# Third layer: the decays over the running sum computed once for 32 heads and broadcast to each tile by DMA

## The reference, cut to what matters

```
dt    = softplus(dt + dt_bias);  Adt = -exp(A_log) * dt          # one number per head and position
A_cum = cumsum(Adt) inside a chunk
Y_diag= (C B^T * exp(segsum(Adt))) @ h                           # inside a chunk
Y_off = (C @ state of the chunks before) * exp(A_cum)            # from the chunks before
y     = Y_diag + Y_off + D * h
g     = y * silu(gate);  out = rmsnorm(g) @ W_out + b_out
```

## Time and profile before

| | |
|---|---|
| median of 3 runs | 1292.9 us (1292.6 to 1293.01) |
| the profiled execution's own time | 1296.16 us |
| its span, first to last instruction | 1294.4 us |
| mean granted TensorE clock | 0.961 |
| busy: PE, weight loads | 1150.9 us (89%), 615.3 us (48%) |
| busy: DVE, ACT, POOL | 939.9 us (73%), 795.5 us (61%), 573.9 us (44%) |
| DMA | 68.48 MB, mean 53 GB/s |

### The profile page before, as it was taken

The page is one execution under the profiler, slowest core; times in us unless marked ns, Lnnn a source line. Parts: engine busy times, 40 slices in busy tenths (PEclk is TensorE's granted clock), DMA queues, the critical chain, the costliest instruction groups (busy, mean ns, idle before and its releaser), DMA issues.

```text
span 1294.4 us, 14453 instructions
## 1 busy us (share of the span) xinstructions
PE 1150.9 (89%) x4948; PEld 615.3 (48%) x4948; DVE 939.9 (73%) x1361; ACT 795.5 (61%) x1089; POOL 573.9 (44%) x310
## 2 busy tenths in 40 slices
PE   5777999999989999998489999999999999797887
PEld 1332344444344444444266666666666666322554
DVE  4667999999955545345689999998999999323354
ACT  4567666767543334226668888888888888335542
POOL 9002899898816756230014544554454455300000
PEclk8889999999989999898699999999999999798999
DMA  3001555555422111100000000000000000000000
GB/s 121 1 1 58 192 197 178 191 180 180 174 105 82 50 41 41 41 21 0 2 15 15 15 21 15 15 22 15 15 14 22 16 15 8 1 0 1 1 1 33
DMA packets 31111, 68.48 MB, mean 53 GB/s; under 512 B 6101, under 2 KB 12022, under 8 KB 30774
## 3 DMA queue, kind: packets, MB, share of 16 engines
q1 hardware_dynamic: 31038, 67.56, 16.1%
HBM read 65.25 MB, written 1.51 MB: 52 GB/s over the span
## 4 chain that ended last, share of the span: by engine, by line
PE 41%; DVE 30%; ACT 15%; issue 7%; POOL 6%; DMA 1%; DVEq 0%; SPq 0%; POOLq 0%; ACTq 0%
DVE work L1542 7%; DVE work L1561 6%; DVE work L656 4%; PE ps L1006 4%; PE ps L1196 4%; PE ps L1022 3%; PE ps L1014 3%; POOL work L717 3%; ACT work L1403 3%; DVE yd L1606 3%; ACT work L1398 3%; PE ps L1237 2%; DVE work L1609 2%; PE ps L437 2%; ACT ps L553 2%
## 5 line engine op out<-in xcount | busy, mean ns | idle before, releaser
L1670 POOL TENSOR_TENSOR ssum<-ssum,rs 128x1024 f32<-128x1024 f32 x32 | 77.1, 2410 | 221.3 <-DVE work L1542 219.0
L656 DVE TENSOR_TENSOR_SCAN work<-ps,work 128x1024 f32<-128x1024 f32 x64 | 146.6, 2291 | 8.3
L1542 DVE SCALAR_TENSOR_TENSOR work<-work,w_t 128x1024 f32<-128x1024 f32 x96 | 123.3, 1285 | 24.0 <-ACT work L1403 21.7
L437 PE MATMUL ps<-work,ident 128*128 128x512 f32 x256 | 121.7, 598 | 5.6 <-POOL work L717 5.4
L996 POOL TENSOR_TENSOR work<-work,ssum 128x1024 f32<-128x1024 f32 x32 | 76.2, 2388 | 110.1 <-DVE work L1085 57.7
L1085 DVE TENSOR_TENSOR work<-work,ps 128x512 f32<-128x512 f32 x64 | 43.8, 687 | 99.8 <-PE ps L1014 99.8
L553 ACT ACTIVATE ps<-work,A 128x1024 f32<-128x1024 f32 x64 | 71.6, 1118 | 72.4 <-DVE work L656 72.3
L1064 ACT ACTIVATE work<-ps 128x512 f32<-128x512 f32 x64 | 38.1, 597 | 115.4 <-PE ps L1006 115.4
L717 POOL TENSOR_TENSOR work<-work 128x1024 f32<-128x1024 f32 x42 | 99.1, 2362 | 13.6 <-DVE work L656 12.3
L1678 POOL TENSOR_TENSOR yd<-yd,work 128x896 f32<-128x896 f32 x32 | 67.1, 2097 | 70.7 <-DVE work L1609 70.7
L1585 DVE SCALAR_TENSOR_TENSOR work<-work,ps 128x64 f32<-128x64 f32 x384 | 79.4, 275 | 6.3
(11 more groups left out here) (347 smaller groups left out, 2587.5 us busy)
## 6 DMA issues: line engine op xcount, KB each, us to landing
work<-bc_rows SPq DMA_DIRECT2D x42, 512.0 KB, 3.5
yd<-bc_rows SPq DMA_DIRECT2D x22, 512.0 KB, 3.6
rs<-w_rows SPq DMA_DIRECT2D x32, 256.0 KB, 4.2
ssum<-share_rows SPq DMA_DIRECT2D x32, 256.0 KB, 3.2
w_t<-in_tile_w SPq DMA_DIRECT2D x32, 195.5 KB, 2.4
work<-in_w SPq DMA_DIRECT2D x1, 2048.0 KB, 7.9
shared<-in_f SPq DMA_DIRECT2D x3, 512.0 KB, 6.1
work<-in_x SPq DMA_DIRECT2D x4, 256.0 KB, 3.7
```

The lines of the kernel that those rows point to most:

```text
L437: mm = pe.matmul(ps[:, YACC + h, :], ident[:, :], HS[u % 4][:, h * BL:(h + 1) * BL], start=(n == 0), stop=(n == DS - 1))
L656: dve.tensor_tensor_scan(h, flat_pair(DABANK), h, 0.0, ALU.mult, ALU.add).then_inc(m0["scan"], 1)
L1542: c = dve.scalar_tensor_tensor(HC[u], HP[:, tap:tap + SEQ], par(u, "taps", tap), HC[u], ALU.mult, ALU.add)
L1670: pool.tensor_tensor(ssum[:, b, :], ssum[:, b, :], rs[:, :, :].rearrange("p k t -> p (k t)"), ALU.add).then_inc(m2["ss"], 1)
```

## The change

- `spread_sums` (PE, two matmuls per tile), `decays_out` (ACT, one exponential of 128x896 per tile) and the selector `sel2` with its memset and three selections are gone, and with them PE's wait on `sdo` ahead of `within_chunks`.
- Ahead of the loop ACT computes the exponential of the transposed running sums once, in four instructions of 32x512, into `rtf[0:32]`. They stand behind the copies of the middle parts, and the high part's copies are issued up to two blocks earlier. The fourth stands ahead of `pad_h(0, 0)`.
- SP stores `rtf[0:32]` into a DRAM scratch `sdo_rows` in two DMAs (one per sequence), and for each tile issues two DMAs that broadcast one row of 896 numbers each to 64 partitions of `Y`. In the loop these wait for `outp` and `sqr` of the tile that had that half of `Y` before, and they stand ahead of `load_tile(n + 2)` and `load_rows(n + 2)` on the queue.
- DVE's L1609 waits for the landing of these DMAs and no longer for ACT.

```diff
+            def store_decays(b):
+                sp.wait_ge(m2["sdo"], (b + 1) * NB // BATCH)
+                here = slice(b * SEQ, (b + 1) * SEQ)
+                sp.dma_start(sdo_rows[:, here], rtf[0:H2, here]).then_inc((m2["sdo_rows0"], m2["sdo_rows1"])[b], 16)
+
+            def load_decays(n):
+
+                b, t = divmod(n, CT)
+                if n >= 2:
+                    sp.wait_ge(m2["outp"], n - 1)
+                    sp.wait_ge(m2["sqr"], n - 1)
+                for h in range(2):
+                    sp.dma_start(Y[n % 2][h * P2:(h + 1) * P2, P:],
+                                 sdo_rows[2 * t + h:2 * t + h + 1, b * SEQ + P:(b + 1) * SEQ].to_broadcast([P2, SEQ - P])).then_inc(
+                                     (m2["sdo_in0"], m2["sdo_in1"])[n % 2], 16)
+
             load_tile(0)
             load_tile(1)
+            store_decays(0)
             sp.wait_ge(m2["rows_const"], 1)
             sp.wait_ge(m2["act"], m2["neg"] + NB)
             load_rows(0)
             load_rows(1)
+            store_decays(1)
+            sp.wait_ge(m2["sdo_rows0"], 16)
+            load_decays(0)
+            load_decays(1)
+            sp.wait_ge(m2["sdo_rows1"], 16)
             for n in range(CT * BATCH - 2):
+                if n >= 1:
+                    load_decays(n + 1)
                 sp.wait_ge(m2["hc"], n + 1)
                 sp.wait_ge(m2["wo"], n + 1)
                 load_tile(n + 2)
                 sp.wait_ge(m2["arg"], 4 * n + 4)
                 load_rows(n + 2)
+            load_decays(CT * BATCH - 1)
...
-            def spread_sums(n, b, t):
-
-                pe.wait_ge(m2["L"], 4 * n + 4)
-                for h in range(2):
-                    mm = pe.matmul(ps[:, BACK + h, :], sel2[:, 2 * t:2 * t + 2, :].rearrange("k a p -> k (a p)"),
-                                   parts[:, b * SEQ + h * BL:b * SEQ + (h + 1) * BL], start=True, stop=True)
-                mm.then_inc(m2["sdo_mm"], 1)
...
             def within_chunks(n):
-                pe.wait_ge(m2["sdo"], n + 1)
                 pe.wait_ge(m2["M"], n + 1)
...
-            def decays_out(n, u):
-                act.wait_ge(m2["sdo_mm"], n + 1)
-                if n >= 2:
-                    act.wait_ge(m2["outp"], n - 1)
-                    act.wait_ge(m2["sqr"], n - 1)
-                act.activation(Y[u][:, P:], flat2(BACK)[:, P:], ACT.Exp).then_inc(m2["sdo"], 1)
...
+            def middle(k):
+                act.wait_ge(m2["mid"], k + 1)
+                act.activation(blk(parts[32:64, :], k), part_tmp[0:H2, k % 2, :], ACT.Copy).then_inc(m2["act"], 1)
+                act.activation(blk(rtf[0:H2, :], k), ps[0:H2, 4 + k, :], ACT.Exp).then_inc(m2["sdo"], 1)
...
-            for k in range(NB):
-                act.wait_ge(m2["pe"], m2["cumT"] + 1)
+            act.wait_ge(m2["pe"], m2["cumT"] + 1)
+            for k in range(NB):
                 act.activation(blk(parts[0:32, :], k), ps[0:H2, 4 + k, :], ACT.Copy).then_inc(m2["act"], 1)
-                act.wait_ge(m2["mid"], k + 1)
-                act.activation(blk(parts[32:64, :], k), part_tmp[0:H2, k % 2, :], ACT.Copy).then_inc(m2["act"], 1)
+                if k >= 1:
+                    middle(k - 1)
+            middle(NB - 1)
             pad_h(0, 0)
...
-                dve.wait_ge(m2["sdo"], n + 1)
+                dve.wait_ge((m2["sdo_in0"], m2["sdo_in1"])[u], 32 * (n // 2 + 1))
                 dve.wait_ge(m2["yoff"], 2 * n + 2)
...
-            for t in (ident_b, mask_q, zero, sel, sel2):
+            for t in (ident_b, mask_q, zero, sel):
                 pool.memset(t[:, :] if len(t.shape) == 2 else t[:, :, :], 0.0)
...
-            for t, w in ((sel2, P2), (sel, P)):
-                for k in range(3):
...
+            for k in range(3):
+                ins = pool.affine_select(sel[:, :, :], sel[:, :, :], [[-1, H2], [0, P]], ALU.not_equal, 1.0,
+                                         base=-H2 * k, channel_multiplier=1)
```

More of the change, by code:

```diff
@@ L147, in build @@
         sel = selectors[0:96, :, :]
-        sel2 = sb("sel2", [96, H2, P2], BF16)
         selr2 = sb("selr2", [4 * E, E, HE], BF16)
@@ L215, in build @@
                     dve="row:1 dt_biased:1 bc_conv:2 dt:1 adt:1 acum:1 dec_sub:1 parts:4 bc_conv1:2 gt_out:4 s_out:4",
-                    each="mid bc_pad bc_tap w_in0 w_in1 h_mm h_pad h_tap g_mm sg conv hc tr hdt hdd rows_const rows0 rows1 arg L sdo_mm sdo st first_state rec M yoff ydiag yd ystar y_sum y sqr ss wo outp first_out")
+                    each="mid bc_pad bc_tap w_in0 w_in1 h_mm h_pad h_tap g_mm sg conv hc tr hdt hdd rows_const rows0 rows1 arg L sdo sdo_rows0 sdo_rows1 sdo_in0 sdo_in1 st first_state rec M yoff ydiag yd ystar y_sum y sqr ss wo outp first_out")
         f2 = stages("f2", pe="logit:1 picked_T:1 y:4", act="sig:1 y_out:4 g:4", dve="picked:1 x_out:4", each="rt_out h gelu wbc hw")
@@ L224, in build @@
         share_rows = nc.dram_tensor("share_rows", [E, T], F32, kind="Internal").ap()
+        sdo_rows = nc.dram_tensor("sdo_rows", [H2, T], F32, kind="Internal").ap()
         bc_rows = nc.dram_tensor("bc_rows", [2 * DS, T], F32, kind="Internal").ap()
@@ L1147, in build @@
         STAIRS = 12
+        HI_AT, MID_AT = (1, 2, 4, 6), (3, 5, 7, 8)
         two = lambda k: ps[:, k:k + 2, :]
@@ L1292, in step @@
                     shares(m, b1, 1)
-                    spread_sums(m, b1, t1)
                 if t == 0:
@@ L1353, in l2_pe @@
             shares(0, 0, 1)
-            spread_sums(0, 0, 0)
             pe.wait_ge(m2["dve"], m2["gt_out"] + NB)
@@ L1474, in step @@
             def step(n, b, t, u):
-                decays_out(n, u)
                 more = n + 1 < CT * BATCH
@@ L1529, in l2_dve @@
                 r, tb = rs[0:H2, k % 2, :], part_tmp[0:H2, k % 2, :]
-                dve.wait_ge(m2["act"], m2["hi_mid"] + 2 * k + 1)
+                dve.wait_ge(m2["act"], m2["hi_mid"] + HI_AT[k])
                 own(dve.tensor_tensor(r, ps[0:H2, 4 + k, :], blk(parts[0:32, :], k), ALU.subtract))
@@ L1533, in l2_dve @@
                 dve.wait_ge(m2["mid"], k + 1)
-                dve.wait_ge(m2["act"], m2["hi_mid"] + 2 * k + 2)
+                dve.wait_ge(m2["act"], m2["hi_mid"] + MID_AT[k])
                 dve.tensor_tensor(blk(parts[64:96, :], k), r, tb, ALU.subtract).then_inc(m2["dve"], 1)
@@ L1979, in _ @@
             pool.affine_select(mask_q[:, :], mask_q[:, :], [[-1, P]], ALU.is_ge, -BIG, base=0, channel_multiplier=1)
-            for t, w in ((sel2, P2), (sel, P)):
-                for k in range(3):
[L1983 to L1988, removed]
+            for k in range(3):
+                ins = pool.affine_select(sel[:, :, :], sel[:, :, :], [[-1, H2], [0, P]], ALU.not_equal, 1.0,
+                                         base=-H2 * k, channel_multiplier=1)
+                if k == 2:
+                    ins.then_inc(const["ready"], 1)
+                else:
+                    own(ins)
             l0_pool(pool, own)
```

## The result

The changed kernel takes 1299.58 us (median of 19 runs, 1295.03 to 1302.87) against 1293.82 us (19 runs, 1288.72 to 1297.63) on the same chips: ratio 1.0038, 95% interval 1.0027 to 1.0049. It is slower by some 0.4%; the forecast was 1279.1 us, faster. The profiled execution took 1302.87 us, its span 1301.2 us. What happened is by its mechanism the rival "the weights come late and the kernel is slower", at a smaller size than its 1316.5 us.

The account below looks back on a forecast made before the run. The loop's step was taken to be bound by a chain through PE, ACT and DVE, with spread_sums a link. Terms -13.0 - 1.4 + 0.6 = -13.8 us took 1292.9 to 1279.1 us; own range 1276 to 1282, 8 in 10 1275 to 1287.

Parts of the forecast that it names:

- the weights come late and the kernel is slower: Rival, SP queue in the loop: weights land at X = 5.92 us, step 14.89 us, 1316.5 us in all; chance 0.05.
- What bounds a step: Third layer's loop: a 14.02 us step is a chain through PE, ACT and DVE, with spread_sums a link, decays_out not.
- PE without spread_sums: PE in the loop: project_h starts 0.42 us earlier in 31 tiles, -13.0 us.
- the two long steps with the clearing of the accumulator save the same: Loop steps that clear the accumulator: led by project_h too, so each saves the same 0.42 us.
- DVE's new wait: DVE L1609 in the loop: decays have 14.0 us and land 3.5 us after issue, so it costs nothing.
- What is queued behind on SP: SP queue in the loop: next tile's weights, behind the decay loads, land 0.4 us inside the budget; cost nothing.
- X: Time from sum_out's end to the weights' landing: taken as 4.2 us, budget 4.63; when over it, step is 8.97 + X.
- "a little late" rival: SP queue in the loop: weights land at X = 4.82 us, step 13.79 us, 1284.6 us in all; chance 0.14.
- The prediction's second estimate of X: SP queue: from 2.0 us fixed plus bytes over 436 GB/s, after 0.84 us of issuing, X of 3.5 to 4.4 us.
- The start: Program start: less POOL work lets DVE's fourth L260 end at 25.2 us instead of 28.2; -1.4 us, bounds 0 and -3.0.
- Ahead of the loop: ACT before the loop: the fourth exponential, a 32x512 pass, stands right ahead of pad_h(0, 0); +0.6 us.
- The sum: Whole kernel: -13.0 - 1.4 + 0.6 = -13.8 us, from 1292.9 to 1279.1 us.

Follow-up runs that it names:

- with the weights first: Changed kernel with SP issuing load_tile and load_rows ahead of load_decays in each iteration: 1279.57 us, ratio to before 0.9883; repeated, 1278.41 us, ratio 0.9884.
- the wait alone: Changed kernel loading decays for tiles 0 and 1 only, SP's wait for outp and sqr kept ahead of load_tile: 1281.9 us, step 13.59 us.

## Why the prediction was wrong

- **What bounds a step:** right. A chain through PE, ACT and DVE, `spread_sums` a link, `decays_out` not. Both were put back alone and did what was said (14.02 and 13.59 us).
- **PE without spread_sums, 0.42 us for 31 tiles:** right as a size, 14.02 - 13.59 = 0.43 us. In the changed kernel only the second step shows it; with the weights first every usual step does. That "the two long steps with the clearing of the accumulator save the same" was wrong for the one of step 16, 16.50 us in both: PE's wait of 0.50 us for ACT L1488 ahead of L1266 takes in what the matmuls leave.
- **DVE's new wait:** right, no wait of DVE for a decay load appears in the list.
- **What is queued behind on SP, "cost nothing, with a thin margin":** this is the step that failed. The mechanism, the cycle 8.97 + X and the point from which it costs (X of 5.05) were right; X was mis-sized, 4.2 us for a measured 5.35 in the step shown (median 5.24). Three parts of it: the two issues and the gap took 1.25 us, where I took 0.92 from loads of 128 partitions; the weights landed 3.96 us after their own issue (median 3.8), where I had 3.24; and PE's start behind the landing (0.14 us) was left out. Besides, PE's part of the step is 9.07 us for 8.97, because project_h takes 1.96 us for 1.88 when it starts on the landing; that its first weight load can no longer run ahead of it is the likely reason, which no run isolated. My 3.5 us for 459 KB was taken as if both loads went out at once (they land 3.7 us after their own issue, and the second is issued 0.55 us after the first), while the trace had a row of three DMAs whose last one landed 3.9 us after its own issue; I used the difference of the two landings and not the value itself. The "a little late" rival used it and was still 0.5 us short (4.82 for 5.35), mostly by the issue and the start. The prediction's second estimate of X, 3.5 to 4.4 us, fell short of the measured value as well.
- **Late a little, late and slower:** in the step shown 9.07 + 5.35 = 14.42 us is the whole step, and the medians give 9.05 + 5.24 = 14.29 us where the median step is 14.34. The loop became 7 us longer (the first convolutions of tiles 1 and 31 are 432.1 us apart, before 424.8). The price of the slower rival (1316.5 us) was for the worst landing, X = 5.92 us, in every step; the measured X is 0.6 us less.
- **The start, -1.4 us:** right up to 31 us (0.69 us for the fourth L260, and 1.9 us by L481); whether the chain behind keeps it is not shown, either way.
- **Ahead of the loop, +0.6 us:** right, measured +0.5; the fourth exponential (636.79, L1453) stands between the middle part and pad_h:

```profile
636.79 0.59 ACT L1453 ACTIVATE rtf<-ps 32x512 f32<-32x512 f32 x1
637.29 1.09 ACT L1413 ACTIVATE work<-ps,w_t 128x1024 f32<-128x1024 f32 x1
```

From the first matmul of the transposed sums to pad_h it is 14.46 us, before 13.97: +0.5 us.

- **The sum:** with the weights first the kernel does what the sum said of the changed one, 1279.57 and 1278.41 us for 1279.1, though against a before of 1293 to 1295 us, so by 14.5 to 15.1 us and not by the 13.8 forecast. The loop accounts for 12.5 us of that (the same two convolutions are 412.3 us apart for 424.8). The other 2 us or so are inside the intervals, which reach 3 us to either side, and no run assigns them to the start or to anything else; that the two times agree to half a microsecond is in part luck.

## What to carry to other kernels

A new DMA on a queue can cost those behind it twice: their issue waits for its semaphores and its issue time, and their landing waits for its bytes. Here the wait alone cost nothing (13.59 us); the issue time and the bytes together used up the margin. Before a load with a long lead is put behind one that waits for late work, write down for each load of the queue when it can be issued and when it is due, and order them so that a load never stands behind a wait later than its own: here moving two lines made 1.0038 into 0.988. And where a margin is a tenth of the term it is taken from, take the landing of the nearest *row of DMAs* from its own issue, not a sum of differences; the thin margin was the prediction's real content.

## What was not expected of the hardware

- Two broadcast loads of 64 partitions hold the issuing engine for 1.14 us (0.50 and 0.59 us), one of 128 partitions with the same bytes for 0.33 us. With rows of 1792, 3584 and 4096 bytes it is the same 1.14 us.
- One load whose source is two rows, each repeated 64 times, into 128 partitions delays a 195.5 KB load behind it to 10.9 us, against 3.8 us behind a load of one row repeated 128 times, at a DMA share of 0.13, what two busy engines of 16 give.
- Kernels that are alike up to 127 us differ there by as much as 2.9 us (125.4 to 128.3 us for the first L656 in twelve profiles), with granted clocks of 0.87 to 0.91 on the way. A gain of 1.4 to 2.7 us at 31 us, which all twelve have, can't be followed through that by single profiles.
